# Layer norm statistics of two graphs by one batch-norm instruction

## The chip, the cores and the metric

The kernel runs on one core of one Trainium2 chip. The metric is the device time of one execution in microseconds (us); shorter is better. A core has five engines that run in parallel, each through its own instructions in order, and wait for one another on semaphores: TensorE (PE, with its weight loads PEld), VectorE (DVE), ScalarE (ACT), GpSimd (POOL) and SyncE (SP), which here only starts transfers.

## The reference, cut to what matters

The input is `x`, 128 graphs of 128 nodes with 128 features, an adjacency matrix for each graph, and the weights of four layers with a residual sum:

```python
def _layernorm(x, axis=-1, eps=1e-05):
    m = jnp.mean(x, axis=axis, keepdims=True)
    v = jnp.var(x, axis=axis, keepdims=True)
    return (x - m) / jnp.sqrt(v + eps)
...
    x = x + _L0_gnn_ref(_layernorm(x, axis=-1), adj, ...)   # five groups of nodes, two graph convolutions each
    x = x + _L0_ffn_ref(_layernorm(x, axis=-1), ...)        # 8 experts, the best 2 of each node
    x = x + _L1_gnn_ref(_layernorm(x, axis=-1), adj, ...)   # one graph convolution
    x = x + _L1_ffn_ref(_layernorm(x, axis=-1), ...)        # shared MLP + 4 experts, the best 2
```

So each layer begins with a layer norm over the 128 features of every node. The statistics of these four layer norms are all that the change touches.

## The kernel before, in words

`x` stays in SBUF for the whole kernel as `xtok` [128 nodes, 128 graphs, 128 features]: a partition holds one node number of all graphs, and the 128 features of one graph are 128 adjacent 4-byte words of it. The next graph lies 512 bytes further. There are four parts in time, each a block in which every engine runs its own loop:

- **Graph stage** (0 to about 235 us). `R = 4` tiles of the group convolutions are one group turn (16 turns, tile `xg`, phases `first`, `middle`, `back` on successive turns). From turn `LAG = 8` on, blocks of `RG = 8` graphs go through the phases `sel_`, `second`, `third`, `logits`, `search` (16 blocks): VectorE adds the convolution's rows to `xtok` (L645), takes statistics of the eight graphs (L630, L635), and later searches the two best experts. So there are turns with group statistics alone, turns with both, and turns with node statistics alone. VectorE's program is the loop `for t in TURNS` (L613 to L767), in the order in which it is written. The variance goes to GpSimd, which raises it to the power -0.5 (L408, L415), and comes back for `dinv`, `dsc`, `xsb` (L698 to L704) or `gnb` (L763).
- **Sort** of nodes by expert (to about 320 us) and the **expert stage** (to about 818 us) hold no layer norm statistics.
- **Last stage** (from 818 us). Thirty-two turns of `R = 4` graphs, plus four that fill and drain it (`turns5`, a `Fori` loop of two turns for each pass). In turn j VectorE adds the experts' rows to graphs of turn j (L1629), takes statistics of turn j-1 for the graph convolution (`k = 0`, L1659 to L1674), adds the convolution's result for turn j-2 and takes statistics again (`k = 1`, L1704 to L1718), and does the routing and gating of turns j-3 and j-4 between these. GpSimd's program for a turn is: 4 gathers of expert rows, `roots(.., 0)`, 4 gathers, `roots(.., 1)` (L1372 to L1390). `roots(.., k)` waits for `pre[k]`, and VectorE waits for its result at L1690 and L1755.

Statistics of one graph are two instructions: `bn_stats` (in the profile BATCH_NORM_STATS2) takes the 128 features and writes six numbers for each partition: count, mean and count times variance of the elements at even places, and the same three of those at odd places. `bn_aggr` (BATCH_NORM_AGGREGATE) joins the two halves and writes mean and variance. Then one `tensor_scalar` adds 1e-5 for the whole turn.

```python
nc.vector.bn_stats(st[k][:, r, :], row(n, r))             # L1636, for each graph
...
last = nc.vector.bn_aggr(mv[k][:, r, :], st[k][:, r, :])  # L1644, for each graph
...
nc.vector.tensor_scalar(pre[k][:, :], mv[k][:, :, 1], 1e-5, None, ALU.add)
```

Of the kernel before, what the change touches and what calls it, by code (L numbers as in the profile page):

```python
# [21 lines left out]
ALU = mybir.AluOpType  # L22
# [3 lines left out]
P = 128  # L26
B = 128
N = P
D = P
R = 4  # L30
# [71 lines left out]
def build(nc, x_tok, x_grp, a_grp, w_grp, fus, wg, bg, w_exp, a_t, w_gcn, b_gcn, mask_t,  # L102
# [8 lines left out]
    with top:  # L111
# [28 lines left out]
        def turns4(eng, n, body):  # L140
# [6 lines left out]
            for j in range(n, n + 3):  # L147
                body(j - j % 2, j % 2, False, j < n + 1, j < n + 2, True)

        def turns5(eng, n, body):  # L150

            for j in range(n + 4):
                body(j - j % 2, j % 2, j < n, 1 <= j < n + 1, 2 <= j < n + 2, 3 <= j < n + 3, j >= 4)
# [14 lines left out]
        passed = sem("passed")  # L168
# [33 lines left out]
        with ExitStack() as ctx:  # L202
# [18 lines left out]
            wb = alloc(ctx, "wb", [P, NGB])  # L221
            st = [alloc(ctx, f"st{p}", [P, R, 6]) for p in range(2)]
            mv = [alloc(ctx, f"mv{p}", [P, R, 2]) for p in range(2)]
            pre = [alloc(ctx, f"pre{p}", [P, 2 * R]) for p in range(2)]
# [17 lines left out]
            tv = [alloc(ctx, f"tv{k}", [P, RG]) for k in range(3)]  # L242
            gst = alloc(ctx, "gst", [P, RG, 6])
            gmv = [alloc(ctx, f"gmv{p}", [P, RG, 2]) for p in range(2)]
            gpre = [alloc(ctx, f"gpre{p}", [P, RG]) for p in range(2)]
# [71 lines left out]
            with nc.Block() as block:  # L317
# [264 lines left out]
                def _(dve):  # L582
# [30 lines left out]
                    for t in TURNS:  # L613
# [14 lines left out]
                        def stats(ks):  # L628
                            for k in ks:
                                last = nc.vector.bn_stats(gst[:, k, :], xtok[:, RG * b + k, :])  # L630
                            return last

                        def averages(ks):
                            for k in ks:
                                last = nc.vector.bn_aggr(gmv[u][:, k, :], gst[:, k, :])  # L635
                            return last
# [10 lines left out]
                        if first:  # L647
                            dve.wait_ge(loaded[p], 32 * (t // 2) + 32)
                            for k in range(R):
                                last = nc.vector.bn_stats(st[p][:, k, :], xg[p][:, k, :])  # L650
                            last.then_inc(stat_s, 1)
                            dve.wait_ge(stat_s, t + 1)
                            for k in range(R):
                                last = nc.vector.bn_aggr(mv[p][:, k, :], st[p][:, k, :])
                            last.then_inc(mv_s, 1)
                            dve.wait_ge(mv_s, t + 1)
                            nc.vector.tensor_scalar(pre[p][:, 0:R], mv[p][:, :, 1], 1e-5, None, ALU.add)
                            dve.wait_ge(deg_done, t + 1)
# [12 lines left out]
                        if second:  # L671
                            dve.wait_ge(x1_ready, b + 1)
                            stats(range(2))
                        if search:
                            dve.wait_ge(lg_ready, c + 2)
                            step(largest(tv[0], lt))
                        if second:
                            stats(range(2, 5))
                        if search:
                            after(1)  # L680
                            step(same(wd[:, :, :], lt, tv[0]))
                        if second:
                            stats(range(5, RG)).then_inc(gstat_s, 1)
                        if search:
# [10 lines left out]
                        if first:  # L695
# [7 lines left out]
                            dve.wait_ge(dinv_s, 4 * t + 3)  # L703
                            nc.vector.scalar_tensor_tensor(xsb[p][:, :], mv[p][:, :, 0], -1.0, dsc[p][:, :],  # L704
                                                           ALU.mult, ALU.mult).then_inc(xsb_ready, 1)
                            dve.sem_inc(dinv_s, 1)
                        if back:
# [3 lines left out]
                                                    ALU.mult).then_inc(zs_ready, 1)  # L711
                        if second:
                            dve.wait_ge(gstat_s, b + 1)
                            averages(range(R))
                        if search:
                            after(3)
                            step(largest(tv[2], wd))
                        if second:
                            averages(range(R, RG)).then_inc(gmv_s, 1)
                        if search:  # L720
                            m0 = mask[0][:, RG * c:RG * c + RG, :]
                            m1 = mask[1][:, RG * c:RG * c + RG, :]
                            after(4)
                            step(same(m0, wd, tv[2]))
                        if second:
                            dve.wait_ge(gmv_s, b + 1)
                            nc.vector.tensor_scalar(gpre[u][:, :], gmv[u][:, :, 1], 1e-5, None, ALU.add)\
                              .then_inc(gpre_ready, 1)
# [32 lines left out]
                        if second:  # L761
                            dve.wait_ge(groot_done, b + 1)
                            nc.vector.scalar_tensor_tensor(gnb[u][:, :], gmv[u][:, :, 0], -1.0, groot[u][:, :],  # L763
                                                           ALU.mult, ALU.mult).then_inc(gnb_ready, 1)
# [480 lines left out]
        with ExitStack() as ctx:  # L1245
# [14 lines left out]
            idx = [alloc(ctx, f"idx{p}", [P, 2, R], I32) for p in range(2)]  # L1260
            st = [alloc(ctx, f"st_l{k}", [P, R, 6]) for k in range(2)]
            mv = [alloc(ctx, f"mv_l{k}", [P, R, 2]) for k in range(2)]
            pre = [alloc(ctx, f"pre_l{k}", [P, R]) for k in range(2)]
# [73 lines left out]
            with nc.Block() as block:  # L1337
# [229 lines left out]
                def _(dve):  # L1567
# [48 lines left out]
                    def body(i, p, complete, norm, aggregate, hidden, finish):  # L1616
# [29 lines left out]

                        def variance(n, k):
                            dve.wait_ge(ln[k], 2 * n + 2)
                            nc.vector.tensor_scalar(pre[k][:, :], mv[k][:, :, 1], 1e-5, None, ALU.add)\  # L1649
                              .then_inc(pre_ready[k], 1)  # L1650

                        if norm:
# [5 lines left out]
                            dve.sem_inc(passed, 1)  # L1658
                            for r in range(R):  # L1659
                                stats(j - 1, 0, r)  # L1660
# [4 lines left out]
                        if norm:  # L1665
                            averages(j - 1, 0)
                        if hidden:
# [19 lines left out]
                        if norm:  # L1687
# [4 lines left out]
                            dve.wait_ge(rd_s, 2 * j - 1)  # L1692
                            nc.vector.scalar_tensor_tensor(nbm[:, :], mv[0][:, :, 0], -1.0, rd[:, :],
                                                           ALU.mult, ALU.mult).then_inc(rd_s, 1)
# [9 lines left out]
                        if aggregate:  # L1704
                            dve.wait_ge(x3_ready, j - 1)
                            dve.sem_inc(passed, 1)
                            for r in range(R):
                                stats(b, 1, r)
# [3 lines left out]
                        if aggregate:  # L1712
                            averages(b, 1)
                        if hidden:
# [38 lines left out]
                        if aggregate:  # L1753
                            dve.wait_ge(root_done[1], j - 1)
                            nc.vector.scalar_tensor_tensor(nb[1][:, :], mv[1][:, :, 0], -1.0, root[1][:, :],  # L1755
                                                           ALU.mult, ALU.mult).then_inc(nb_ready[1], 1)
# [116 lines left out]
```

## Time and profile before

| what | value |
|---|---|
| median of 3 runs | 1334.93 us (1333.78 to 1335.29) |
| profiled execution, its own time | 1336.69 us |
| its span, first to last instruction | 1334.8 us |
| granted TensorE clock, mean over the span | 0.937 |
| busy: PE, DVE, ACT, POOL | 89%, 85%, 75%, 63% of the span |
| chain that ended last | begins at 818 us: shares of PE 16%, DVE 10%, POOL 6%, issue 5% of the span |

The profile records one execution. Busy shares are averages over parts with different limits; the chain that ended last is followed back from the last instruction and here covers only the last stage. In the views by line, a group is all instructions of one line and shape. In the views in order of time, consecutive instructions of one line are merged (x4 is four of them, from the start of the first to the end of the last); a bracket gives the idle time of the engine before them and who ended it.

### The profile page before, as it was taken

How to read it: one execution, taken by the hardware profiler on the slowest of the kernel's cores; microseconds unless marked ns; L12 is line 12 of the kernel's file. 1: busy time of each engine (PE TensorE's matmuls, PEld its weight loads, DVE VectorE, ACT ScalarE, POOL GpSimd, SP SyncE). 2: the span in 40 equal slices, each digit the busy share in tenths (PEclk: the TensorE clock that was granted, in tenths of full speed). 3: DMA queues.
4: the chain of work that ended last, by engine and by line, in shares of the span. 5: the costliest groups of instructions: out<-in, count | busy, mean ns of one | idle time of the engine just before them, and what ended most of it. 6: DMA issues, size and time to landing. Idle time of an engine off the chain costs nothing. (4 is left out here: it accounts for less than half of the span.)

```text
span 1334.8 us, 21838 instructions
## 1 busy us (share of the span) xinstructions
PE 1193.2 (89%) x6288; PEld 870.6 (65%) x6288; DVE 1137.0 (85%) x4033; ACT 997.9 (75%) x1947; POOL 843.4 (63%) x781
## 2 busy tenths in 40 slices
PE   5889988364999999999999993499999999999998
PEld 4767757253777777777777772366666666666665
DVE  4778998897899998999999996589898988989885
ACT  3457666493999999999999993477777777777774
POOL 3345555675777777777777763676666666667630
PEclk9999975576999999999999997599999999999999
DMA  5578764400222332322222262123222322222210
GB/s 183 200 234 265 210 184 137 169 1 19 69 80 78 78 78 78 80 79 80 79 78 79 77 77 62 54 62 85 65 70 69 84 67 70 76 76 68 68 48 24
DMA packets 137642, 124.89 MB, mean 94 GB/s; under 512 B 15630, under 2 KB 117106, under 8 KB 136371
## 3 DMA queue, kind: packets, MB, share of 16 engines
q1 hardware_dynamic: 119219, 88.06, 21.4%
q0 software_dynamic: 18304, 35.44, 11.8%
q8 instruction: 51, 0.84, 0.3%
q14 instruction: 68, 0.56, 0.1%
HBM read 83.78 MB, written 39.67 MB: 92 GB/s over the span
## 5 line engine op out<-in xcount | busy, mean ns | idle before, releaser
L1069 POOL DMA_INDIRECT exg<-xln_scratch,eidx x284 | 315.2, 1110 | 124.3 <-issue 69.3
L1362 POOL DMA_INDIRECT yg<-expert_rows_scratch,idx x256 | 253.4, 990 | 95.2 <-issue 72.5
L1208 DVE TENSOR_TENSOR ehl<-ehr,ehh 128x512 fp32r<-128x512 f32 x284 | 194.7, 686 | 28.7 <-ACT ehh L1093 28.5
L1090 ACT ACTIVATE ehr<-p_eh,bc 128x512 f32<-128x512 f32 x284 | 195.9, 690 | 25.1 <-PE p_eh L1128 17.0
L1093 ACT ACTIVATE ehh<-ehr 128x512 fp32r<-128x512 f32 x284 | 179.6, 633 | 9.0
L1369 POOL TENSOR_TENSOR root_l<-pre_l,mhalf 128x4 f32<-128x4 f32 x64 | 66.6, 1041 | 96.9 <-DVE pre_l L1649 96.2
L1126 PE MATMUL p_ey<-ehh,wh 128*128 128x512 f32 x284 | 124.8, 439 | 1.0 <-DVE ehl L1208 0.8
L1126 PE MATMUL p_eh<-exh,wh 128*128 128x512 f32 x284 | 124.0, 437 | 1.5 <-DVE exl L1203 1.5
L1128 PE MATMUL p_eh<-exh,wl 128*128 128x512 f32 x284 | 112.6, 396 | 0.0
L1127 PE MATMUL p_eh<-exl,wh 128*128 128x512 f32 x284 | 112.2, 395 | 0.0
L1128 PE MATMUL p_ey<-ehh,wl 128*128 128x512 f32 x284 | 111.9, 394 | 0.0
L1127 PE MATMUL p_ey<-ehl,wh 128*128 128x512 f32 x284 | 111.5, 393 | 0.0
L1405 ACT ACTIVATE he<-p_lh,be 128x512 f32<-128x512 f32 x128 | 87.8, 687 | 21.9 <-PE p_lh L1479 21.9
L1190 DVE TENSOR_TENSOR wl<-wall,wh 128x512 fp32r<-128x512 f32 x142 | 98.5, 693 | 4.9
L1629 DVE SCALAR_TENSOR_TENSOR xtok<-yg,prob,xtok 128x128 f32<-128x128 f32 x256 | 73.0, 346 | 19.3 <-DMA yg<-expert_rows_scratch,idx 16.7
L1126 PEld LDWEIGHTS p_ey<-ehh,wh 128*128 128x128 f32 x284 | 53.1, 187 | 47.6 <-DVE ehl L1208 40.7
L1475 PE MATMUL p_lh<-x4h,w1h 128*128 128x512 f32 x160 | 77.2, 483 | 1.4 <-ACT he L1405 1.3
L1411 ACT ACTIVATE xn<-xtok,nb,rd 128x128 f32<-128x128 f32 x128 | 52.8, 482 | 28.2 <-DVE nb L1702 28.1
L1553 PEld LDWEIGHTS p_out<-w,rc 128*128 128x128 f32 x512 | 59.6, 191 | 18.0 <-DVE rc L1731 17.9
L1553 PE MATMUL p_out<-w,rc 128*128 128x128 f32 x512 | 65.4, 281 | 5.1 <-DVE rc L1731 2.6
L911 PE MATMUL p_id<-hh,lc 128*128 128x284 f16 x224 | 40.5, 349 | 32.4 <-DVE hh L978 32.4
L1469 PE MATMUL p_lh<-he,w 128*64 128x512 f32 x256 | 68.8, 617 | 0.0
(228 smaller groups left out, 3152.8 us busy)
## 6 DMA issues: line engine op xcount, KB each, us to landing
expert_rows_scratch<-eyo SPq DMA_DIRECT2D x71, 256.0 KB, 2.3
xtok<-in_x_tok SPq DMA_DIRECT2D x8, 1024.0 KB, 6.8
an<-in_a_t SPq DMA_DIRECT2D x16, 512.0 KB, 4.5
xln_scratch<-xl SPq DMA_DIRECT2D x16, 512.0 KB, 4.3
at<-in_a_t SPq DMA_DIRECT2D x32, 256.0 KB, 3.0
out<-outx SPq DMA_DIRECT2D x32, 256.0 KB, 2.6
wj<-in_w_grp SPq DMA_DIRECT2D x16, 321.0 KB, 4.5
exg<-xln_scratch,eidx POOLq DMA_INDIRECT x284
```

What stands on the lines that cost most here:

```text
L1069: pool.indirect_dma_start(out=xg[p][:, k, :], out_offset=None, in_=xln_d, in_offset=bass.IndirectOffsetOnAxis(ap=idx[p][:, k:k + 1], axis=0))\
L1090: nc.scalar.activation(hr[c % 2][:, :], p_h[c][:, :], ACT.Relu, bias=bc[p][:, c:c + 1])\
L1093: nc.scalar.activation(hh[:, c, :], hr[c % 2][:, :], ACT.Copy).then_inc(hh_ready, 1)
L1126: nc.tensor.matmul(dst, w_hi, a_hi, start=start, stop=False)
L1127: nc.tensor.matmul(dst, w_hi, a_lo, start=False, stop=False)
L1128: return nc.tensor.matmul(dst, w_lo, a_hi, start=False, stop=stop)
L1190: nc.vector.tensor_tensor(wl[p][:, cols], w[:, cols], wh[p][:, cols].bitcast(F32), ALU.subtract).then_inc(ready, 1)
L1208: nc.vector.tensor_tensor(hl[:, c, :], hr[c % 2][:, :], hh[:, c, :].bitcast(F32), ALU.subtract)\
L1362: pool.indirect_dma_start(out=yg[p][:, c, k, :], out_offset=None, in_=y_d, in_offset=bass.IndirectOffsetOnAxis(ap=idx[p][:, c, k:k + 1], a ...
L1405: nc.scalar.activation(dst, p_h[u % 2][:, :], ACT.Relu, bias=bias).then_inc(h_ready, 1)
L1475: nc.tensor.matmul(dst, w1h[:, e, :], x4h[:, :], start=True, stop=False)
L1553: last = nc.tensor.matmul(p_out[:, k, :], rc[u][:, k * P:(k + 1) * P], w3[:, u, :], start=False, stop=(u == 1 and k == R - 1))
```

## The change

One `bn_stats` now reads the rows of two graphs, elements of the two in turn: feature 0 of the first graph, feature 0 of the second, feature 1 of the first, and so on, 256 elements. Its even places are then the first graph and its odd places the second, so the six numbers that it writes are the statistics of two whole graphs. There is no `bn_aggr` any more; the variance is the third number divided by 128, which the `tensor_scalar` that adds 1e-5 now does too, and later users read the mean from `st` in place of `mv`. The waits between `bn_stats` and `bn_aggr` and between `bn_aggr` and `tensor_scalar` become one between `bn_stats` and `tensor_scalar`. In the graph stage, the eight instructions that were spread between steps of the search as 2, 3 and 3 become four, spread as 1, 1 and 2.

```diff
+        def two_rows(dst, src):
+            return nc.vector.bn_stats(dst.rearrange("p r s -> p (r s)"), src.rearrange("p r d -> p d r"))
...
                         def stats(ks):
                             for k in ks:
-                                last = nc.vector.bn_stats(gst[:, k, :], xtok[:, RG * b + k, :])
-                            return last
-
-                        def averages(ks):
-                            for k in ks:
-                                last = nc.vector.bn_aggr(gmv[u][:, k, :], gst[:, k, :])
+                                last = two_rows(gst[u][:, k:k + 2, :], xtok[:, RG * b + k:RG * b + k + 2, :])
                             return last
...
-                            for k in range(R):
-                                last = nc.vector.bn_stats(st[p][:, k, :], xg[p][:, k, :])
+                            for k in range(0, R, 2):
+                                last = two_rows(st[p][:, k:k + 2, :], xg[p][:, k:k + 2, :])
                             last.then_inc(stat_s, 1)
                             dve.wait_ge(stat_s, t + 1)
-                            for k in range(R):
-                                last = nc.vector.bn_aggr(mv[p][:, k, :], st[p][:, k, :])
-                            last.then_inc(mv_s, 1)
-                            dve.wait_ge(mv_s, t + 1)
-                            nc.vector.tensor_scalar(pre[p][:, 0:R], mv[p][:, :, 1], 1e-5, None, ALU.add)
+                            nc.vector.tensor_scalar(pre[p][:, 0:R], st[p][:, :, 2], 1.0 / D, 1e-5, ALU.mult, ALU.add)
...
-                            stats(range(2))
+                            stats((0,))
...
-                            stats(range(2, 5))
+                            stats((2,))
...
-                            stats(range(5, RG)).then_inc(gstat_s, 1)
+                            stats((4, 6)).then_inc(gstat_s, 1)
...
-                        if second:
-                            dve.wait_ge(gstat_s, b + 1)
-                            averages(range(R))
...
-                        if second:
-                            averages(range(R, RG)).then_inc(gmv_s, 1)
...
-                            dve.wait_ge(gmv_s, b + 1)
-                            nc.vector.tensor_scalar(gpre[u][:, :], gmv[u][:, :, 1], 1e-5, None, ALU.add)\
+                            dve.wait_ge(gstat_s, b + 1)
+                            nc.vector.tensor_scalar(gpre[u][:, :], gst[u][:, :, 2], 1.0 / D, 1e-5, ALU.mult, ALU.add)\
                               .then_inc(gpre_ready, 1)
...
-                        def stats(n, k, r):
-                            ins = nc.vector.bn_stats(st[k][:, r, :], row(n, r))
-                            if r == R - 1:
-                                ins.then_inc(ln[k], 1)
-
-                        def averages(n, k):
-                            dve.wait_ge(ln[k], 2 * n + 1)
-                            dve.sem_inc(passed, 1)
-                            for r in range(R):
-                                last = nc.vector.bn_aggr(mv[k][:, r, :], st[k][:, r, :])
+                        def stats(n, k):
+                            for r in range(0, R, 2):
+                                last = two_rows(st[k][:, r:r + 2, :], xtok[:, R * n + r:R * n + r + 2, :])
                             last.then_inc(ln[k], 1)
 
                         def variance(n, k):
-                            dve.wait_ge(ln[k], 2 * n + 2)
-                            nc.vector.tensor_scalar(pre[k][:, :], mv[k][:, :, 1], 1e-5, None, ALU.add)\
+                            dve.wait_ge(ln[k], n + 1)
+                            nc.vector.tensor_scalar(pre[k][:, :], st[k][:, :, 2], 1.0 / D, 1e-5, ALU.mult, ALU.add)\
                               .then_inc(pre_ready[k], 1)
```

The calls of `averages` in the last stage go too, and the three places that read the mean (`xsb`, `gnb`, and `nbm` and `nb` of the last stage) read it from `st` or `gst`.

## Rows read from the trace of the kernel before

**Rows 1.** Windows: stretch, length, busy PE PEld DVE ACT POOL, granted clock, DMA share, GB/s.

```profile
183.00:222.00 39.00, 33.93 (x134) 24.23 (x134) 33.25 (x185) 22.21 (x53) 22.51 (x12) 0.56 0.62 177
853.00:1310.00 457.00, 444.05 (x2469) 300.29 (x2470) 401.38 (x1977) 347.65 (x798) 295.25 (x296) 0.99 0.25 68
```

**Rows 2.** VectorE by line: xcount | busy us, mean ns of one | idle before.

```profile
L1636 DVE BATCH_NORM_STATS2 st_l<-xtok 128x6 f32<-128x128 f32 x256 | 55.5, 279 | 2.4
...
L1644 DVE BATCH_NORM_AGGREGATE mv_l<-st_l 128x2 f32<-128x6 f32 x256 | 24.0, 156 | 2.8
```

**Rows 3.** Chain that ended last, both ends of 17 last-stage turns: start us, us, what.

```profile
1049.69 2.06 PE p_lh L1469 x6
...
1299.24 2.06 PE p_lh L1469 x6
```

**Rows 4.** VectorE in order of time, one last-stage turn: start us, us, engine, line, operation.

```profile
1110.26 0.86 DVE L1636 BATCH_NORM_STATS2 st_l<-xtok 128x6 f32<-128x128 f32 x4
1111.04 0.68 DVE L1663 TENSOR_TENSOR x4l<-x4t,x4h 128x512 fp32r<-128x512 f32 x1
1111.63 0.37 DVE L1644 BATCH_NORM_AGGREGATE mv_l<-st_l 128x2 f32<-128x6 f32 x4
...
1112.04 0.17 DVE L1649 TENSOR_SCALAR pre_l<-mv_l 128x4 f32<-128x4 f32 x1
...
1114.70 0.87 DVE L1636 BATCH_NORM_STATS2 st_l<-xtok 128x6 f32<-128x128 f32 x4
1115.49 0.15 DVE L1711 TENSOR_REDUCE sv<-sm 128x4 f32<-128x16 f32 x1
...
1116.22 0.16 DVE L1614 TENSOR_TENSOR sm<-sm,sv 128x16 f32<-128x16 f32 x1
1116.42 0.17 DVE L1608 TENSOR_REDUCE sv<-sm 128x4 f32<-128x16 f32 x1
...
1119.40 0.16 DVE L1755 SCALAR_TENSOR_TENSOR nb<-mv_l,root_l 128x4 f32<-128x4 f32 x1 [0.35 <-POOL root_l L1369]
```

**Rows 5.** GpSimd in order of time, same turn.

```profile
1112.29 1.03 POOL L1369 TENSOR_TENSOR root_l<-pre_l,mhalf 128x4 f32<-128x4 f32 x1 [2.51 <-DVE pre_l L1649]
...
1118.33 1.04 POOL L1369 TENSOR_TENSOR root_l<-pre_l,mhalf 128x4 f32<-128x4 f32 x1
```

**Rows 6.** TensorE weight loads in order of time, same turn.

```profile
1115.00 0.18 PEld L1489 LDWEIGHTS p_cb<-cwd,selp 32*128 32x128 f32 x1 [0.37 <-issue]
...
1117.66 1.86 PEld L1553 LDWEIGHTS p_out<-w,rc 128*128 128x128 f32 x16 [0.58 <-DVE rc L1731]
```

**Rows 7.** VectorE by line again: instructions that give the price of an element.

```profile
L958 DVE TENSOR_REDUCE pos_f<-wide 128x128 f32<-128x1024 f32 x2 | 2.4, 1219 | 0.1
L953 DVE TENSOR_TENSOR posf<-p_rank,base_r 128x512 f32<-128x512 f32 x2 | 2.2, 1079 | 0.6 <-PE p_rank L903 0.6
L1581 DVE TENSOR_REDUCE selp<-selraw 32x256 fp32r<-32x1024 f32 x1 | 1.9, 1873 | 0.0
```

**Rows 8.** VectorE, a graph-stage turn with group statistics alone.

```profile
55.74 0.86 DVE L650 BATCH_NORM_STATS2 st<-xg 128x6 f32<-128x128 f32 x4
...
57.20 0.16 DVE L659 TENSOR_SCALAR nz<-p_thin 128x4 f32<-128x4 f32 x1
```

**Rows 9.** TensorE in the same turn.

```profile
56.22 0.95 PE L521 MATMUL p_thin<-ones,ag 128*128 128x1 f32 x8
```

**Rows 10.** VectorE, a graph-stage turn with both kinds of statistics.

```profile
127.94 0.47 DVE L630 BATCH_NORM_STATS2 gst<-xtok 128x6 f32<-128x128 f32 x2
...
129.75 0.20 DVE L686 TENSOR_TENSOR wd<-wd,cf 128x64 f32<-128x64 f32 x1
```

**Rows 11.** TensorE in the same turn.

```profile
132.50 1.16 PE L567 MATMUL p_z<-zs,ag 128*128 128x128 f32 x8 [0.92 <-DVE zs L709]
```

**Rows 12.** VectorE, a graph-stage turn with node statistics alone.

```profile
189.55 0.17 DVE L763 SCALAR_TENSOR_TENSOR gnb<-gmv,groot 128x8 f32<-128x8 f32 x1 [0.25 <-POOL groot L415]
...
193.91 0.17 DVE L727 TENSOR_SCALAR gpre<-gmv 128x8 f32<-128x8 f32 x1
```

More of the change, by code:

```diff
@@ L221, in build @@
             wb = alloc(ctx, "wb", [P, NGB])
-            st = [alloc(ctx, f"st{p}", [P, R, 6]) for p in range(2)]
-            mv = [alloc(ctx, f"mv{p}", [P, R, 2]) for p in range(2)]
+            st = [alloc(ctx, f"st{p}", [P, R, 3]) for p in range(2)]
             pre = [alloc(ctx, f"pre{p}", [P, 2 * R]) for p in range(2)]
@@ L242, in build @@
             tv = [alloc(ctx, f"tv{k}", [P, RG]) for k in range(3)]
-            gst = alloc(ctx, "gst", [P, RG, 6])
-            gmv = [alloc(ctx, f"gmv{p}", [P, RG, 2]) for p in range(2)]
+            gst = [alloc(ctx, f"gst{p}", [P, RG, 3]) for p in range(2)]
             gpre = [alloc(ctx, f"gpre{p}", [P, RG]) for p in range(2)]
@@ L703, in _ @@
                             dve.wait_ge(dinv_s, 4 * t + 3)
-                            nc.vector.scalar_tensor_tensor(xsb[p][:, :], mv[p][:, :, 0], -1.0, dsc[p][:, :],
+                            nc.vector.scalar_tensor_tensor(xsb[p][:, :], st[p][:, :, 1], -1.0, dsc[p][:, :],
                                                            ALU.mult, ALU.mult).then_inc(xsb_ready, 1)
@@ L717, in _ @@
                             step(largest(tv[2], wd))
-                        if second:
-                            averages(range(R, RG)).then_inc(gmv_s, 1)
-                        if search:
                             m0 = mask[0][:, RG * c:RG * c + RG, :]
@@ L762, in _ @@
                             dve.wait_ge(groot_done, b + 1)
-                            nc.vector.scalar_tensor_tensor(gnb[u][:, :], gmv[u][:, :, 0], -1.0, groot[u][:, :],
+                            nc.vector.scalar_tensor_tensor(gnb[u][:, :], gst[u][:, :, 1], -1.0, groot[u][:, :],
                                                            ALU.mult, ALU.mult).then_inc(gnb_ready, 1)
@@ L1260, in build @@
             idx = [alloc(ctx, f"idx{p}", [P, 2, R], I32) for p in range(2)]
-            st = [alloc(ctx, f"st_l{k}", [P, R, 6]) for k in range(2)]
-            mv = [alloc(ctx, f"mv_l{k}", [P, R, 2]) for k in range(2)]
+            st = [alloc(ctx, f"st_l{k}", [P, R, 3]) for k in range(2)]
             pre = [alloc(ctx, f"pre_l{k}", [P, R]) for k in range(2)]
@@ L1658, in body @@
                             dve.sem_inc(passed, 1)
-                            for r in range(R):
-                                stats(j - 1, 0, r)
+                            stats(j - 1, 0)
                         if hidden:
@@ L1664, in body @@
                               .then_inc(x4l_ready, 1)
-                        if norm:
-                            averages(j - 1, 0)
                         if hidden:
@@ L1692, in body @@
                             dve.wait_ge(rd_s, 2 * j - 1)
-                            nc.vector.scalar_tensor_tensor(nbm[:, :], mv[0][:, :, 0], -1.0, rd[:, :],
+                            nc.vector.scalar_tensor_tensor(nbm[:, :], st[0][:, :, 1], -1.0, rd[:, :],
                                                            ALU.mult, ALU.mult).then_inc(rd_s, 1)
@@ L1706, in body @@
                             dve.sem_inc(passed, 1)
-                            for r in range(R):
-                                stats(b, 1, r)
+                            stats(b, 1)
                         if hidden:
@@ L1711, in body @@
                             router(nc.vector.tensor_reduce(sv[1][:, :], sm[1][:, :, :], AX.X, ALU.add))
-                        if aggregate:
-                            averages(b, 1)
                         if hidden:
@@ L1754, in body @@
                             dve.wait_ge(root_done[1], j - 1)
-                            nc.vector.scalar_tensor_tensor(nb[1][:, :], mv[1][:, :, 0], -1.0, root[1][:, :],
+                            nc.vector.scalar_tensor_tensor(nb[1][:, :], st[1][:, :, 1], -1.0, root[1][:, :],
                                                            ALU.mult, ALU.mult).then_inc(nb_ready[1], 1)
```

## The prediction

> **What bounds the kernel now.** I read first what the turns of each part wait for, then the prices. The chain that ended last covers the last stage alone, and there one turn follows the next in (1299.24 - 1049.69) / 17 = 14.68 us [rows 3]. Two loops of that length run side by side.
>
> Loop A goes over VectorE and GpSimd: `pre` of the first norm (L1649) ends at 1112.21, GpSimd, idle for 2.51 us until then, starts `root` at 1112.29, issues four gathers, and ends the second `root` at 1118.33 + 1.04 = 1119.37 [rows 4, 5]. VectorE, idle for 0.35 us, starts `nb` (L1755) at 1119.40 [rows 4]. From there to the next `pre`, some 7.3 us, VectorE has no idle stretch in the trace. That piece holds the first norm's statistics (L1636 and L1644 after `at`). Both engines wait for each other and nothing between is slack: what VectorE saves between `nb` and `pre` shortens loop A by as much.
>
> Loop B goes over TensorE: it is busy 444 of 457 us [rows 1], and waits for VectorE at one place that the change reaches. The weight load for `p_out` stands 0.58 us until `rc` is there, where other loads after such a switch of product stand 0.37 us with nothing to wait for [rows 6]. So 0.21 us of a turn is VectorE's there. `rc` comes after the second norm's statistics (1114.70) in VectorE's order.
>
> The graph stage has three kinds of turns. With group statistics alone, VectorE is done with `pre` in time, but the next step `nz` needs the degrees: TensorE starts them at 56.22 for 0.95 us, to 57.17, and `nz` starts at 57.20 [rows 8, 9]. TensorE sets the pace; the statistics lie beside it. With both kinds, from about 120 to 158 us, TensorE waits 0.92 us for `zs` [rows 11], which VectorE reaches only after all statistics [rows 10]; these are about three turns. With node statistics alone, VectorE and GpSimd form a loop again (`gnb` waits 0.25 us for `groot`), 193.91 - 189.55 = 4.36 us of which is VectorE's between `gnb` and `gpre` [rows 12]. But from 183 to 222 us TensorE is busy 33.9 of 39 us at a granted clock of 0.56 [rows 1], so only some of these turns follow VectorE.
>
> **The price of the new instruction.** Four `bn_stats` take 0.87 us, the last one 0.28 of it [rows 2, 4]: one starts 0.195 us after the other. The nearest slope of an element is (1219 - 680) / 512 = 1.05 ns, from a reduction of 1024 elements and an operation on 512 [rows 4, 7]. So 0.135 us of the 0.195 is 128 elements and 0.06 is fixed. I call c the pace of the new instruction with 256 elements:
>
> - Lower bound: elements at 1.05 ns, c = 0.27 + 0.06 = 0.33.
> - The new read jumps 512 bytes at each element. `selp` (L1581) is the only VectorE instruction here whose read does that: its innermost index steps over four rows 1024 bytes apart. It takes 1873 ns where the adjacent 1024 elements of L958 take 1219 [rows 7]: 0.64 ns more each, 1.69 ns, c = 0.43 + 0.06 = 0.49.
> - `posf` (L953) jumps with its write, 32 bytes each: 1079 ns for 512 elements where adjacent ones take 680, so 0.78 ns more, 1.83 ns, c = 0.53 [rows 4, 7].
>
> The ends are far apart (0.33 and 0.53), and I take 0.49, the row it is nearest to: a one-source read that changes rows at each element. What speaks for the lower end is that `selp` returns to a row after four elements and the new read after two; no row tells these apart.
>
> The Trainium skill (Vector Engine (DVE) Microarchitecture Reference, "Measured stream behaviour on trn2") says that a port has its full rate only if elements come in runs of two adjacent words, and gives 1.73 ns for a source that hops at every element; by that, the sum below would hardly differ, and `selp` agrees with 1.69. The same section reports one exception, a single read stream alternating between two regions 16 KiB apart at the full rate. That is the shape of this change at another distance, and it is my first rival.
>
> **The change part by part.**
>
> Last stage, first norm (loop A). Before: L1636 to L1663 is 1110.26 to 1111.04 = 0.78, then L1663 to `pre` 1.00 [rows 4]. After: 2c, then L1663 (0.59, to where L1644 stood), L1669 (about 0.12 to the next start), `pre`: 0.71. The `tensor_scalar` with two operations instead of one keeps its length; `pre` waits for statistics that L1663 has long covered. Sum: 2c + 0.71 - 1.78 = 2c - 1.07. With c = 0.49: -0.09 us a turn.
>
> Last stage, second norm (loop B). Before: 1114.70 to 1116.22 = 1.52 [rows 4]. After: 2c, then L1711, its successor and L1614, each of which needs the one before. Such steps start 0.20 apart (1116.22, 1116.42) [rows 4], and the four `bn_aggr` that covered one of these latencies are gone: 2c + 0.40. Sum: 2c - 1.12, with 0.49 -0.14 us, all of it inside TensorE's 0.21.
>
> Both loops shrink, A by less, so a turn gives 0.09, rounded down to 0.08 for what the steps need elsewhere. Over 31 of the 32 turns: -2.5 us. The shorter VectorE program also makes `cwd` wait longer for TensorE; that is idle time off both loops. GpSimd's gathers start with `root` and move with it; their transfers were issued 8 a turn before and are still.
>
> Graph stage. Group statistics: before, start to `pre` 1.31 (0.87, `bn_aggr` 0.38 and two waits); after, 2c plus the tail of the last (0.08) and a wait (0.03) = 2c + 0.11, so -0.22. It counts only in the three mixed turns; in the others `nz` goes on waiting for the degrees. Node statistics: eight at 0.195 with two search steps between, 1.81 us [rows 10]; after, 4c + 0.22, so 4c - 1.59 = +0.37: here the jumping read costs more than two plain ones. In mixed turns the node `bn_aggr` stand in the shadow of TensorE's `p_z`, so dropping them gives nothing: -0.22 + 0.37 = +0.15, three turns, +0.5. In turns with node statistics alone, eight `bn_aggr` go (four start within 0.29, as 0.37 less the last's overlap) but the search steps between them now wait for each other, 0.3 of 0.6 us given back: -0.3 + 0.37 = +0.07, five turns, +0.4.
>
> Sort and expert stage: nothing changes. SyncE's queue has no instruction added or moved.
>
> Sum: -2.5 + 0.5 + 0.4 = -1.6 us. Against the profiled execution's own 1336.69 us that is 1335.1. The median of the runs, 1334.93, is 1.76 below that execution, so I forecast **1333.3 us**.
>
> **The rivals.**
>
> 1. *Alternating reads run at the full rate*, c = 0.33. Loop A shrinks by 1.07 - 0.66 = 0.41, loop B's VectorE part by 0.46, of which 0.21 counts; a little more may lie in the wait for `xn`. TensorE then sets the turn: -0.25 x 31 = -7.8. Mixed turns: -0.54 - 0.27, of which TensorE's 0.92 us of waiting lets some 0.7 count, x3 = -2.1; node turns -0.27 - 0.3, for two turns until TensorE holds: -1.2. Sum -11.1: **1323.8 us**. For it: two rows are fewer than `selp`'s four. Against it: every row with a jump here pays.
> 2. *Slower: the jump costs more than in `selp`.* The point from which loop A grows is 2c = 1.07, c = 0.535, or 1.85 ns an element, just above `posf`'s 1.83. If each element pays `selp`'s surcharge twice, 2.33 ns, c = 0.66: last stage +0.25 x 31 = 7.8, mixed turns (0.12 + 1.05) x 3 = 3.5, node turns 0.75 x 5 = 3.7, sum +15: **1350 us**; just above the threshold it is 1338. For it: `posf` and `selp` already differ, so the surcharge depends on the pattern. Against it: no row of VectorE is above 1.83.
> 3. *The time is saved but not on the path*: full rate, but TensorE's loop B is 14.68 us by itself, the 0.21 us at `rc` turn into another wait. Only the graph stage gives: about **1331.6 us**. For it: TensorE is busy 97% of the stage. Against it: the weight load's extra wait.
>
> **How the numbers follow.** Chances: forecast 0.43, rival 1 0.40, rival 2 0.12, rival 3 0.05. The forecast's own range is 1330.5 to 1337. Less than 0.2% (2.7 us), about what a measurement of this kernel can tell from no change, separates it from before in most of its range: of its 0.43 some 0.05 is faster by more, 0.03 slower by more. With rival 1 (0.40) and part of rival 3 (0.03), faster has 0.48; slower 0.12 + 0.03 = 0.15; same 0.37. The range for 8 in 10 takes in rival 1 and the threshold of rival 2: 1321 to 1338.
>
> **What would show it.** The mean of the new BATCH_NORM_STATS2: 0.58 us for the forecast (0.43 + the 0.145 that a single one has beyond its elements), 0.41 for rival 1, above 0.62 for rival 2. A last-stage turn of 14.60 us (forecast) or 14.43 (rival 1). GpSimd's wait for `pre` barely shorter; the weight load before `p_out` standing about 0.45 us. In mixed turns, TensorE's wait for `zs` should grow slightly, and group-only turns should not move. Wrong would be the prediction if the price of an element is another, since the sum changes sign with it, or if the granted clock of the late graph stage shifts.

## The result, and the profile after

The changed kernel takes 1314.95 us (median of 5 runs, 1314.22 to 1317.83), the kernel before 1334.93 us on the same chip (5 runs, 1333.78 to 1338.93; the three of "Time and profile before" are among them): ratio 0.9846, 95% interval 0.9829 to 0.9863, or some 20 us less, where 1.6 were forecast. The profiled execution after took 1317.83 us, span 1316.0; the span before was 1334.8.

The first row to read is the price. VectorE by line and shape, kernel after (busy us, mean ns of one | idle before):

```profile
L151 DVE BATCH_NORM_STATS2 st_l<-xtok 128x6 f32<-128x256 f32 x128 | 48.8, 423 | 2.4
```

One instruction takes 423 ns where the forecast had 580. Against the old one's 279 ns [rows 2] that is 144 ns for 128 more elements, 1.13 ns each; one alone and two in a row (0.42 and 0.75 us, below) put the pace c at 0.33, the lower bound of the forecast's term.

The chain that ended last, kernel after, both ends of 16 last-stage turns:

```profile
909.17 2.06 PE p_lh L1454 x6
...
1137.43 2.06 PE p_lh L1454 x6
```

A turn is (1137.43 - 909.17) / 16 = 14.27 us against 14.68 [rows 3]: 0.41 us less. Two of the 31 distances between turns lie in the drain of the loop and last as long as before (12.5 and 10.2 us); over the other 29 this is 11.9 us. From the first `cwd` of the stage to the end of the span the two kernels differ by 458.1 - 445.9 = 12.2 us. VectorE in order of time, kernel after, one such turn:

```profile
1110.93 0.75 DVE L151 BATCH_NORM_STATS2 st_l<-xtok 128x6 f32<-128x256 f32 x2
...
1112.27 0.16 DVE L1627 TENSOR_SCALAR pre_l<-st_l 128x4 f32<-128x4 f32 x1
...
1113.59 0.68 DVE L1657 TENSOR_TENSOR cwd<-p_ta,own 32x512 fp32r<-32x512 f32 x1 [0.82 <-PE p_ta L1514]
...
1115.33 0.77 DVE L151 BATCH_NORM_STATS2 st_l<-xtok 128x6 f32<-128x256 f32 x2
...
1116.41 0.17 DVE L1599 TENSOR_TENSOR sm<-sm,sv 128x16 f32<-128x16 f32 x1
...
1119.64 0.16 DVE L1727 SCALAR_TENSOR_TENSOR nb<-st_l,root_l 128x4 f32<-128x4 f32 x1 [0.35 <-POOL root_l L1354]
```

Loop A can be read off. From `nb` to the next `pre` it was 1112.04 + 14.68 - 1119.40 = 7.32 us [rows 4]; now 1112.27 + 14.27 - 1119.64 = 6.90, 0.42 less. The other part, `pre` to `nb` over GpSimd, is 7.37 us where it was 7.36. Before `rc`, the piece from the second statistics to the second router step after them went from 1.52 us [rows 4] to 1116.41 - 1115.33 = 1.08. GpSimd in order of time, kernel after, shows its wait for `pre` 0.43 us shorter than in [rows 5], where the prediction had it barely shorter:

```profile
1112.52 1.04 POOL L1354 TENSOR_TENSOR root_l<-pre_l,mhalf 128x4 f32<-128x4 f32 x1 [2.08 <-DVE pre_l L1627]
```

TensorE around the product for `p_out`, in order of time, first the kernel before, then after:

```profile
1117.12 0.40 PE L1479 MATMUL p_lh<-x4l,w1h 128*128 128x512 f32 x1
1117.66 2.05 PE L1553 MATMUL p_out<-w,rc 128*128 128x128 f32 x16
1119.46 0.48 PE L1475 MATMUL p_lh<-x4h,w1h 128*128 128x512 f32 x1
```

```profile
1117.77 0.40 PE L1464 MATMUL p_lh<-x4l,w1h 128*128 128x512 f32 x1
1118.01 1.95 PE L1538 MATMUL p_out<-w,rc 128*128 128x128 f32 x16
1119.71 0.48 PE L1460 MATMUL p_lh<-x4h,w1h 128*128 128x512 f32 x1
```

From the start of the matmul ahead to the start of `p_out` it was 0.54 us and is 0.24; the sixteen matmuls, start to next start, took 1.80 and take 1.70, since the second `rc` is there in time as well. So TensorE gave 0.40 us, where the prediction allowed it 0.21.

The graph stage: all `gnb` instructions of the kernel after (shortest, median, longest ns, first to last start).

```profile
L749 DVE SCALAR_TENSOR_TENSOR gnb<-gst,groot x16: 159/163/169, 91.2 to 220.0; 128x8 f32<-128x8 f32 x16
```

Before, they ran from 91.0 to 225.2. The first has not moved by more than it varies (90.8 to 91.7 us with the old graph stage, 89.9 to 91.5 with the new one in the experiments below), so the nine turns with group statistics alone, which all come before it, gave little or nothing. Both kinds of statistics stand in seven turns (in the kernel before they begin at 81 to 149 us), not in three. Of the 5.4 us between first and last `gnb`, the six turns from 91 to 158 us give 67.5 - 62.8 = 4.7: one by one 10.20, 11.83, 10.95, 11.64, 11.79, 11.11 us before and 9.60, 10.56, 10.96, 10.43, 10.87, 10.43 after.

Not all of this comes from the cheaper statistics. The windows of these six turns, for the kernel before, for `e3` (an experiment below whose graph stage is the old one) and for the kernel after, columns as in [rows 1]:

```profile
90.98:158.50 67.52, 63.67 (x423) 50.92 (x424) 61.09 (x314) 48.62 (x107) 40.28 (x23) 0.95 0.84 251
90.84:155.82 64.98, 61.99 (x427) 48.90 (x426) 61.26 (x315) 49.51 (x108) 40.31 (x23) 1.00 0.86 260
91.19:154.04 62.85, 60.41 (x425) 48.45 (x424) 56.16 (x206) 48.51 (x107) 40.36 (x23) 1.00 0.90 270
```

At the same granted clock of 1.00 the change is worth 64.98 - 62.85 = 2.1 us there; the other 2.5 separate two executions of one and the same graph stage, at 0.95 and at 1.00. Whether the change itself keeps the clock up is not shown: of the four executions with the old graph stage (before, `e1`, `e3`, `e4`) three were below 1.00 in this stretch, of the nine with the new one (all but `e12`) two. By the mean of these executions the six turns went from 66.4 to 63.2 us and the later ones from 66.7 to 65.5, and the last `gnb` comes 5.0 us earlier (224.4 to 219.4).

A mixed turn and, further up, a turn with group statistics alone, VectorE in order of time, kernel after:

```profile
64.19 0.76 DVE L151 BATCH_NORM_STATS2 st<-xg 128x6 f32<-128x256 f32 x2
64.98 0.17 DVE L649 TENSOR_SCALAR pre<-st 128x4 f32<-128x4 f32 x1
65.65 0.16 DVE L651 TENSOR_SCALAR nz<-p_thin 128x4 f32<-128x4 f32 x1 [0.50 <-PE p_thin L522]
...
136.34 0.42 DVE L151 BATCH_NORM_STATS2 gst<-xtok 128x6 f32<-128x256 f32 x1
...
137.95 0.20 DVE L678 TENSOR_TENSOR wd<-wd,cf 128x64 f32<-128x64 f32 x1
```

`nz` now waits 0.50 us for the degrees: there the saving became idle time, as the prediction said. In the mixed turn the node statistics and the steps between take 137.95 - 136.34 = 1.61 us where they took 1.81 [rows 10]; the forecast's formula 4c + 0.22 gives 1.54 with c = 0.33 and 2.18 with its own 0.49. TensorE's wait for `zs` is gone in the turn where it was 0.92 us [rows 11], and in the one after it it fell from 0.59 us to 0.37.

What holds the kernel now is in the shares of the chain that ended last, by engine, kernel after (PE had 16%, DVE 10%, POOL 6%), and in that chain's order of time within a turn:

```profile
PE 30%; DVE 3%; POOL 3%; issue 1%; DMA 1%; ACT 0%; DVEq 0%; POOLq 0%; ACTq 0%
```

```profile
1113.44 0.12 PE p_ta L1514
1113.57 0.02 issue
1113.59 0.69 DVE cwd L1657
1114.28 0.04 issue
1114.32 0.50 PE p_cb L1474
```

`cwd` is the one piece of VectorE left in a turn of it; all others are TensorE's.

The profiled executions add up: the last `gnb` 5.1 us earlier, the end of the sort 5.6 (318.3 to 312.7 us), the end of the span 18.8. Of the other 13.2, 12.2 lie behind the first `cwd`, in the last stage, and 1.0 between the sort and it, where no instruction is changed.

### The profile page after: what moved, and what is told of

It reads as the page before. It is cut to its first block and busy times, and to the rows that moved or that the text cites. A ratio compares the mean times of both kernels' runs of the same rounds, so it can differ in the third digit from the quotient of the medians.

```text
span 1316.0 us, 21102 instructions
## 1 busy us (share of the span) xinstructions
PE 1187.9 (90%) x6288; PEld 872.2 (66%) x6288; DVE 1095.7 (83%) x3361; ACT 996.7 (76%) x1947; POOL 843.1 (64%) x781
## 3 DMA queue, kind: packets, MB, share of 16 engines
q0 software_dynamic: 18304, 35.44, 12.5%
## 5 line engine op out<-in xcount | busy, mean ns | idle before, releaser
L1055 POOL DMA_INDIRECT exg<-xln_scratch,eidx x284 | 320.6, 1129 | 124.4 <-issue 69.4
L1422 ACT ACTIVATE gr<-p_tb,dm 128x128 f32<-128x128 f32 x128 | 36.6, 369 | 40.6 <-PE p_tb L1506 40.6
L1396 ACT ACTIVATE xn<-xtok,nb,root_l 128x128 f32<-128x128 f32 x128 | 52.7, 482 | 15.2 <-DVE nb L1727 15.2
```

What stands on the lines that cost most here:

```text
L1055: pool.indirect_dma_start(out=xg[p][:, k, :], out_offset=None, in_=xln_d, in_offset=bass.IndirectOffsetOnAxis(ap=idx[p][:, k:k + 1], axis=0))\
L1396: last = nc.scalar.activation(xn[k][:, r, :], xtok[:, bass.ds(R * b + r, 1), :].rearrange("p a d -> p (a d)"), ACT.Identity, scale=scale[: ...
```

## The experiments

The ratios below are to the kernel before on the same chip. The totals of one kernel scatter by up to 15 us between executions on some chips, so each verdict rests first on the length of a last-stage turn, given as the median distance between starts of `cwd`. In the kernel before most turns take 14.63 to 14.74 us, in the kernel after 14.25 to 14.28, and a few in each take 0.3 us more. How much a part without any changed instruction can vary is seen in the one-hot products of the sort, all instructions of that line, here in the kernel after and then in `e4`.

```profile
L897 PE MATMUL p_id<-hh,lc x224: 282/287/461, 252.8 to 313.0; 128*128 128x284 f16 x112
```

```profile
L914 PE MATMUL p_id<-hh,lc x224: 282/338/457, 256.3 to 328.2; 128*128 128x284 f16 x112
```

The same products take 60 us in one and 72 in the other; why is not shown.

**One part at a time.** `e1`: the change in the last stage alone. `e2`: in the graph stage alone. `e3` and `e4`: only in the last stage's first norm (`k = 0`) or only in its second. All four give the other places back their old lines, as here in `stats` for `e3`:

```diff
+                            if k == 1:
+                                for r in range(R):
+                                    last = nc.vector.bn_stats(st[k][:, r, :], row(n, r))
+                            else:
+                                for r in range(0, R, 2):
+                                    last = two_rows(st[k][:, r:r + 2, :], xtok[:, R * n + r:R * n + r + 2, :])
```

> The graph stage as before, both norms of the last stage as after. My theory now, the two loops of the last stage: a turn of 14.27 us in place of 14.68, so 0.41 x 31 = 12.9 us less, 1322 us. The rival, that part of the gain is a shift of the clock or of the transfers that only the whole change brings: less than 9 us.

Measured: 1327.76 against 1340.56 us, ratio 0.9896 [0.9863, 0.9929]; turn 14.27 us; the last `gnb` at 226.5. The last stage alone gives the whole 0.41 us a turn, and the graph stage stands as before.

> The graph stage as after, the last stage as before. By the two traces the last gnb starts 5.2 us earlier and the expert stage 4.1 us earlier, so 1330 us, with a last-stage turn of 14.68 us. The rival, that the late graph stage is TensorE's at a low clock: not more than 3 us.

Measured: 1337.5 us, ratio 0.9974 [0.9948, 0.9999]; turn 14.68; the last `gnb` at 219.7, 5.5 us earlier than before. The two halves are independent and their ratios multiply to 0.987; the whole change has 0.9846, within what their intervals leave open.

> The kernel before with the new statistics in the last stage's first norm alone (loop A's). Theory of the two loops: loop A shrinks by 0.41, but loop B with the old second norm is nearly as long as 14.68 (some turns before ran at 14.63), so a turn of 14.6 us and 1 to 3 us less. The rival, that only loop A counts: a turn of 14.27 us and 13 us less. A second rival, that VectorE's total counts: half of 13, 6.5 us less.

Measured: 1337.98 us, ratio 0.9977 [0.9953, 1.0001]; turn 14.53. TensorE's weight loads in order of time:

```profile
1118.52 1.86 PEld L1556 LDWEIGHTS p_out<-w,rc 128*128 128x128 f32 x16 [0.47 <-DVE rc L1742]
```

Loop A is short and loop B is not: `rc` is still late.

> The kernel before with the new statistics in the last stage's second norm alone (loop B's). Theory: loop A stays at 14.68 us, so nothing (within 1 us), and the load for p_out no longer waits for rc. The rival, that VectorE's total counts: 6.5 us less.

Measured: 1344.14 us, ratio 1.0025 [1.0, 1.005]; turn 14.70. Waits by line, `e4`, 900 to 1280 us: instruction, releaser, total us, count, longest.

```profile
ACT xn L1414 <- DVE nb L1766: 22.8, 26, 0.9
DVE nb L1766 <- POOL root_l L1372: 19.4, 26, 0.8
PE p_tb L1501 <- ACT xn L1414: 9.7, 26, 0.4
```

The wait for `rc` is gone and `nb` waits the more for `root`: 19.4 us where the kernel before has 7.4. What TensorE no longer waits for at `p_out` it now waits for at `xn`, which needs `nb`. Alone, the first norm gives 0.15 us a turn and the second nothing; together 0.41. That is the signature of two loops of nearly one length: with the second norm short the turn stays at loop A's 14.7 us, with the first one short it stops at loop B's 14.5.

**The price by itself.** `e5` puts fourteen groups of four extra instructions ahead of the last stage's turns, each instruction reading 256 elements in another order; nothing else is changed.

```diff
+                    for m in range(4):
+                        nc.vector.bn_stats(pa[:, m, :], xtok[:, 0:2, :].rearrange("p r d -> p (r d)"))
+                    for m in range(4):
+                        nc.vector.bn_stats(pb[:, m, :], xtok[:, 0:2, :].rearrange("p r d -> p d r"))
...
+                    for m in range(4):
+                        nc.vector.bn_stats(pd[:, m, :], xtok[:, 0:4, 0:64].rearrange("p r d -> p d r"))
```

> The kernel after, with 14 groups of four extra VectorE instructions on 256 elements each, put before the turns of the last stage, their results unused. If a read that alternates is free whatever the distance and the number of rows, all bn_stats start 0.33 us apart. If only two rows in turn are free, four and eight rows cost 0.43 + 0.06 = 0.49, and so do the reductions over four rows, while two rows at 512 bytes and at 16 KiB stay at 0.33. If the surcharge of selp came from its kind (a reduction, a 4-byte rounded output), all reads in f32 are free here. Single words 32 bytes apart that are never returned to: 0.53 by posf's row.

VectorE in order of time, from one execution. The `bn_stats`: adjacent words; two rows 512 bytes apart; two rows 16 KiB apart; four rows 512 bytes apart; eight rows; four rows 1024 bytes apart; single words 32 bytes apart. Then a reduction of adjacent words, two rows and four rows, and a `tensor_scalar` of two rows and of adjacent words.

```profile
825.84 1.40 DVE L1786 BATCH_NORM_STATS2 price<-xtok 128x6 f32<-128x256 f32 x4
827.15 1.40 DVE L1788 BATCH_NORM_STATS2 price<-xtok 128x6 f32<-128x256 f32 x4
828.47 1.40 DVE L1790 BATCH_NORM_STATS2 price<-xtok 128x6 f32<-128x256 f32 x4
829.79 2.05 DVE L1792 BATCH_NORM_STATS2 price<-xtok 128x6 f32<-128x256 f32 x4
831.76 2.04 DVE L1794 BATCH_NORM_STATS2 price<-xtok 128x6 f32<-128x256 f32 x4
833.72 2.04 DVE L1796 BATCH_NORM_STATS2 price<-xtok 128x6 f32<-128x256 f32 x4
835.68 2.14 DVE L1798 BATCH_NORM_STATS2 price<-xtok 128x6 f32<-128x256 f32 x4
837.75 1.37 DVE L1800 TENSOR_REDUCE rprice<-xtok 128x64 f32<-128x256 f32 x4
839.04 1.39 DVE L1802 TENSOR_REDUCE rprice<-xtok 128x128 f32<-128x256 f32 x4
840.36 2.04 DVE L1804 TENSOR_REDUCE rprice<-xtok 128x64 f32<-128x256 f32 x4
...
845.12 0.89 DVE L1810 TENSOR_SCALAR wprice<-xtok 128x256 f32<-128x256 f32 x4
845.94 0.88 DVE L1812 TENSOR_SCALAR wprice<-xtok 128x256 f32<-128x256 f32 x4
```

From start to start, a quarter each: 0.33, 0.33, 0.33, then 0.49 for four rows, eight rows and four rows further apart, and 0.52 for the words 32 bytes apart. Two rows in turn cost what adjacent words cost, at 512 bytes and at 16 KiB; four cost (0.492 - 0.06) / 256 = 1.69 ns an element, which is `selp`'s to the digit [rows 7]. The reductions repeat it for adjacent words, two rows and four rows 512 bytes apart. So `selp` was read rightly, and was the wrong row.

The Trainium skill (Vector Engine (DVE) Microarchitecture Reference, "Measured stream behaviour on trn2") states the full rate only for runs of two adjacent words, and the alternation of two regions 16 KiB apart as an exception. The exception agrees with the third row here; its rule does not hold for the second, and the measurement decides.

**The forecast's price in the changed kernel.** `e12` makes the new instruction read the features of each row 32 bytes apart, the two rows still in turn, and changes nothing else; the statistics are the same, since the order of a row's features does not matter to them.

```diff
-            return nc.vector.bn_stats(dst.rearrange("p r s -> p (r s)"), src.rearrange("p r d -> p d r"))
+            return nc.vector.bn_stats(dst.rearrange("p r s -> p (r s)"), src.rearrange("p r (a b) -> p b a r", b=8))
```

> The kernel after with one edit in two_rows: features in steps of eight (0, 8, 16, ... then 1, 9, ...), still of the two graphs in turn, so the same statistics, but each element now lies 32 bytes from the last of its row. If the price of an element is what my forecast got wrong and its sums hold otherwise, this kernel pays 0.49 to 0.53 us for an instruction, the turn is 14.60 to 14.68 us, and the time is that of the forecast, within 3 us of the kernel before. The rival, that the gain is the dropped joining and waits and the price matters little: under 1325 us.

Measured: 1333.93 against 1335.11 us, ratio 0.9994 [0.998, 1.0007]; turn 14.62, most of them 14.57 to 14.66. By line:

```profile
L151 DVE BATCH_NORM_STATS2 st_l<-xtok 128x6 f32<-128x256 f32 x128 | 72.2, 605 | 2.3
```

At a pace of 0.52 (605 ns against the forecast's 580) the kernel lands where the forecast put it: 1.2 us under before, where the forecast said 1.6. That the totals agree so well is partly luck, since the interval is 1.8 us to each side and the split is less good: the last `gnb` comes at 229.4 us, 4.2 late against the profiled execution before, where the prediction's formulas give 1.9 with c = 0.52 (2 x 0.52 - 1.20 + 4 x 0.52 - 1.59 = +0.33 in three mixed turns, +0.19 in five others). The mixed turns are seven, and the granted clock from 91 to 158 us was 0.92 in this execution. In the last stage the formulas give 14.65, and 14.62 was read.

**Joining against reading.** `e11`: in the last stage four plain `bn_stats` in place of the two, and no joining, so that the statistics are those of the even elements alone.

```diff
-                            for r in range(0, R, 2):
-                                last = two_rows(st[k][:, r:r + 2, :], xtok[:, R * n + r:R * n + r + 2, :])
+                            for r in range(R):
+                                last = nc.vector.bn_stats(st[k][:, r, :], row(n, r))
```

> The kernel after, but in the last stage the statistics are again four bn_stats of one graph's 128 adjacent elements, and the joining of their halves is left out, so mean and variance come from the even elements alone. It has the part of the change that drops bn_aggr and not the part that reads two rows in turn. Loop A against before: -0.29 of the -0.41, so a turn of 14.39 us, 4 us over the kernel after. The rival, that the whole gain is the joining and its waits: 14.27.

Measured: 1319.83 against 1333.72 us, ratio 0.9889 [0.9854, 0.9924]; turn 14.36. Of the 0.41 us of a turn, 0.32 come from dropping `bn_aggr` and its wait, and 0.09 from having two instructions in place of four.

**How much slack each loop has now.** `e6`, `e7` and `e8` add one more two-row `bn_stats` (0.33 us) to each turn of the kernel after: ahead of the first norm's statistics (loop A), just before `cwd`, and ahead of the second norm's (before `rc`). The edit of `e7`:

```diff
+                        if norm:
+                            two_rows(xtra[:, :, :], xtok[:, R * (j - 1):R * (j - 1) + 2, :])
                         if finish:
```

> The kernel after with one extra two-row bn_stats (0.33 us) a turn right before the first norm's, on loop A. Theory: all of it shows, a turn of 14.27 + 0.33 = 14.60 us, +10 us over the kernel after. The rival, that TensorE with 97% busy sets the turn: under +3 us.

> The kernel after with the same extra instruction a turn right before cwd, where VectorE idles 0.82 us for TensorE, on neither loop. Theory: a turn of 14.27 us as in the kernel after. The rival, that VectorE's total counts: 14.60 us, +10 us.

> The kernel after with the same extra instruction a turn right before the second norm's, on loop B alone. With the old second norm (0.46 longer) loop B was 14.52 in the run with the first norm alone; with 0.33 in place of 0.46 it is 14.52 - 0.13 = 14.39 us a turn, +4 us over the kernel after. The rival, that loop B has slack beyond that: 14.27. The other, that both loops are equally long: 14.60.

Measured, against 1334.04 us: `e6` 1325.12, ratio 0.9937 [0.9917, 0.9956], turn 14.60; `e7` 1316.09, ratio 0.987 [0.9838, 0.9901], turn 14.27; `e8` 1323.9, ratio 0.9925 [0.9902, 0.9948], turn 14.55. In loop A the 0.33 us show in full; before `cwd` they vanish in VectorE's 0.82 us of waiting for `p_ta`; before `rc` 0.28 of them show, more than I expected. The kernel after has about 0.05 us to spare there and none in loop A.

**Two attempts at more.** `e9` lets GpSimd make the second root after three of the four gathers that stood ahead of it. `e10` moves the addition `at` (0.6 us) out of loop A to just before `cwd`.

```diff
-                        early = R // 2 if isinstance(j, int) and j <= 2 else R
+                        early = R // 2 if isinstance(j, int) and j <= 2 else R - 1
```

> The kernel after with GpSimd's second root moved ahead of the fourth gather of the second four. VectorE waits 0.35 us for it and then reaches nb as soon as its own order allows, so loop A loses at most 0.35: 13.92 us. Theory: loop B, 14.52 less the 0.46 of the second norm = 14.06 us, then sets the turn, 0.2 x 31 = 6 us less than the kernel after. The rival, that loop A is VectorE's own work and GpSimd's wait only its shadow: no change, 14.27. A second rival, that the later fourth gather makes the sum of expert rows wait: slower.

> The kernel after with the addition of the identity to the adjacency (at, 0.61 us of VectorE a turn) moved out of loop A into the place before cwd, where VectorE idles 0.82 us for TensorE and where an extra instruction cost nothing. Loop A: 14.27 - 0.61 = 13.66 us. Loop B, from 14.54 us with 0.33 more before rc: 14.54 - 0.33 = 14.2 us, or a little less. Theory: a turn of 14.1 to 14.2, 2 to 5 us less than the kernel after, 1310 to 1313. The rival: as in the run with the earlier second root, ScalarE begins to stall at places that the profile names no releaser for, a turn of 14.8 us and 15 us more.

`e9`: 1331.75 us, ratio 0.9983 [0.9965, 1.0001] to before, most turns 14.7 to 15.2: some 18 us above 1334.04 x 0.9846, the kernel after on that chip. `nb` no longer waits for `root`; in its place the waits by line, 900 to 1280 us, show

```profile
ACT agt L1414 <- remote: 21.2, 13, 1.6
```

ScalarE is idle for up to 1.6 us before `agt`, once in two turns, with a releaser that the profile calls remote and does not name. The turns between have waits of the same kind before `x4t`, or before `rp` and `x4t`, 1.4 to 2.4 us in all. The four turns from 880 to 1300 us that have none take 14.22 to 14.26 us, so these waits are what makes the others long; where they come from stays open. Without them the turn would still not be the 14.06 that was expected. `e10`: 1314.48 against 1333.72 us, ratio 0.9852 [0.9824, 0.9881], turn 14.27, the same as the kernel after, where 14.1 to 14.2 was expected. Its chain that ended last, in order of time, has the piece that the kernel after has:

```profile
1111.27 0.12 PE p_ta L1514
1111.39 0.02 issue
1111.42 0.69 DVE cwd L1658
1112.11 0.04 issue
1112.15 0.49 PE p_cb L1474
```

Loop A was shortened, to 6.54 us from `nb` to `pre`, and nothing came of it: loop B over TensorE is 14.27 us long by itself. (`e6` and `e8` say that the loops are equally long in the kernel after, `e10` that shortening one does not help.) No version beat the kernel after by a measurable amount.

## Why the prediction was wrong

**What bounds the kernel: right.** Two loops side by side, A over VectorE and GpSimd, B over TensorE with `rc` as its door to VectorE. `e3` and `e4` show that neither alone gives what both do. They also show that B was not quite of A's length: 14.53 us against 14.7.

**The price of the new instruction: the step that failed.** "I take 0.49, the row it is nearest to: a one-source read that changes rows at each element." It measured 0.33 in the kernel and in `e5`. The nearest row goes round four places, this one round two, and `e5` shows the step between these (0.33 for two rows, 0.49 for four; three were not measured); the prediction had named that difference and given it the smaller chance, by little (0.40 against 0.43). `e12`, with the kernel otherwise unchanged, gives back nearly all of the 20 us.

**The formulas: right in the last stage.** 2c - 1.07 for loop A is -0.41 with c = 0.33; -0.42 was read. 2c - 1.12 before `rc` is -0.46; -0.44 was read.

**How much TensorE can follow: mis-sized, also in rival 1.** The prediction took 0.37 of the 0.58 us at the `p_out` load [rows 6] as unavoidable, from another load that stands so long with nothing to wait for. After the change this load shows no idle time in 21 of 27 turns, and 1.3 us in all in the other six. All of the 0.30 us there was VectorE's, and the second `rc` hid another 0.10 within the sixteen matmuls, which a view of starts would have shown. So rival 1 forecast 0.25 us a turn and 0.41 came, in the last stage 7.8 us against 12.2: 4.4 of the 8.9 us by which its 1323.8 was high.

**The graph stage: the mechanism right, the count of turns wrong, the size right at one clock.** Turns with group statistics alone did not move noticeably. Mixed turns are seven and not about three. Rival 1's 2.1 us for them is what the six behind the first `gnb` gave at a granted clock of 1.00 (2.1); between the profiled executions they gave 4.7, since the one before ran at 0.95 there. Three turns at 0.7 and six uneven ones coming to the same sum is luck. Later turns gave 0.7 between the profiled executions and 1.2 in the mean of all, against rival 1's 1.2. The clock that the prediction named as its risk was that of the late graph stage, and it hardly shifted (0.56 to 0.59 from 183 to 222 us).

**The rest.** By the stages' own rows the change is worth 12.2 + 5.0 = 17 us, and the medians differ by 20 with an interval of about 2.3 to each side. The other 3 are not assigned; the unchanged sort varies by more than that. The cost at nothing of the longer wait before `cwd` was right (`e7`). Rival 2 (slower) fell with the price. Rival 3 (TensorE's loop 14.68 us long by itself) is refuted by the turn of 14.27; it describes the kernel after, though, which stands on TensorE at 14.27 (`e10`).

## What to carry to other kernels

When a price is the term that decides the sign or the size, look for what distinguishes the row at hand from the case (here: among how many places the read goes round), and weight the rival by that, not by how near the row looks. A bracket of idle time before an instruction is only partly "unavoidable" if the same instruction in other turns has none: compare starts, and look inside groups of matmuls for a second wait. Where two loops have nearly one length, change both or expect little, and after that see which one is left: here one more cut in loop A has nothing to give. And before a gain is read off two profiled executions, compare their granted clocks in the stretch: here half of the mixed turns' 4.7 us goes with it.

## What the hardware showed unexpectedly

A 4-byte read that alternates between two rows costs VectorE nothing in `bn_stats`, at 512 bytes and at 16 KiB (0.33 us for 256 elements, as adjacent), nor in a reduction at 512 bytes (0.33); a round of four or eight rows costs 1.69 ns an element. A `tensor_scalar` of 256 elements in `e5` takes (845.94 - 845.12) / 4 = 0.21 us even when it alternates, where `bn_stats` takes 0.33. A row's features 32 bytes apart, two rows in turn, cost 0.52 (`e12`), as in a single row (`e5`). And one gather issued after a root in place of before it (`e9`) brought ScalarE into waits that no named engine releases and made most turns 0.5 to 0.9 us longer; this was not resolved.
